# Aggregation passes of a four-layer graph network: 64 gather buffers in the feature buffer, indices copied 32 at a time, one-hots made eight in one instruction

## The reference

```python
# GCN, twice:  h = h @ W
agg = jax.ops.segment_sum(h[src] * norm[:, None], dst, num_segments=n)
# SAGE, once:  hn = layernorm(h) * gamma + beta
msg_sum = jax.ops.segment_sum(hn[src], dst, num_segments=n)
out = hn @ W_self + (msg_sum / jnp.maximum(deg, 1.0)[:, None]) @ W_neigh + b
```

## Time and profile before

| | us |
|---|---|
| median of the runs | 18431.7 |
| span of the profiled execution (first to last instruction) | 21138.5 |
| three aggregation passes in it (13177 to 15662, 15807 to 18300, 18564 to 21052) | about 7470 |
| two attention passes in it (759 to 3800, 4160 to 7050) | about 5900 |
| edge network in it (7490 to 12830) | about 5300 |
| the last block in it (21052 to 21138.5) | about 87 |

### The profile page before, as it was taken

One profiled execution on the slowest core, in us unless ns is written; L12 is line 12 of the kernel. 1 busy time (PEld: TensorE's weight loads), 2 busy tenths in 40 slices (PEclk: granted clock), 3 DMA queues, 4 the chain that ended last, 5 costly groups with the idle time before them and its releaser, 6 DMA issues. The chain is left out here.

```text
span 21138.5 us, 217919 instructions
## 1 busy us (share of the span) xinstructions
PE 9540.9 (45%) x37741; PEld 7773.1 (37%) x37741; DVE 8097.6 (38%) x29032; ACT 1416.9 (7%) x3852; POOL 12654.5 (60%) x12031
## 2 busy tenths in 40 slices
PE   0333333322222278888888885333333333333334
PEld 0222222222222266666666663232322332223233
DVE  6344444343434533333333334333333333543334
ACT  0000000000000111111111111000000000000000
POOL 1555555355555268888888882666646666356665
PEclk6555555555555566666666667555555555555556
DMA  2321221311111255555555553111121111111111
GB/s 70 57 48 48 48 48 46 48 38 40 38 39 38 62 108 106 106 106 106 106 106 106 106 105 95 44 44 44 44 68 44 44 44 44 40 51 44 44 44 48
DMA packets 1753968, 1328.70 MB, mean 63 GB/s; under 512 B 528762, under 2 KB 1576227, under 8 KB 1750312
## 3 DMA queue, kind: packets, MB, share of 16 engines
q0 software_dynamic: 570240, 778.48, 18.2%
q1 hardware_dynamic: 1182704, 530.37, 10.0%
q10 hardware_dynamic: 728, 17.33, 0.2%
HBM read 1134.48 MB, written 230.11 MB: 65 GB/s over the span
## 5 line engine op out<-in xcount | busy, mean ns | idle before, releaser
L692 POOL DMA_INDIRECT wk<-tab,idx x4992 | 4782.6, 958 | 3237.1 <-ACT idx L682 1767.1
L704 PE MATMUL PS<-wk 128*128 128x128 f32 x9984 | 2731.3, 445 | 4889.3 <-DVE wk L716 3724.4
L854 POOL DMA_INDIRECT hs<-tab_g,wk x3328 | 3232.1, 971 | 2663.0 <-ACT wk L815 1650.2
L704 PEld LDWEIGHTS PS<-wk 128*128 128x128 f32 x9984 | 2241.0, 319 | 5380.3 <-DVE F L726 3232.2
L1471 POOL DMA_INDIRECT agg<-F x1664 | 2632.9, 1582 | 515.0 <-issue 505.2
L918 PE MATMUL PS<-wk,hs 128*128 128x128 f32 x6656 | 1628.7, 416 | 2738.3 <-DVE wk L939 1302.6
L726 DVE TENSOR_TENSOR F<-F,PS 128x128 f32 x4992 | 1442.5, 289 | 3638.0 <-issue 1626.0
L918 PEld LDWEIGHTS PS<-wk,hs 128*128 128x128 f32 x6656 | 1379.9, 302 | 2991.3 <-DVE wk L939 1348.3
L1460 POOL DMA_INDIRECT F<-tab,idx x1664 | 1642.9, 987 | 720.5 <-issue 487.5
L960 DVE TENSOR_TENSOR F<-F,PS 128x126 f32 x3328 | 952.0, 286 | 2310.0 <-issue 1773.6
L716 DVE TENSOR_SCALAR wk<-iota_row,locT 128x128 f32<-128x128 f32 x4992 | 1240.2, 304 | 1154.0 <-issue 1120.2
(11 more groups left out here) (287 smaller groups left out, 8190.1 us busy)
## 6 DMA issues: line engine op xcount, KB each, us to landing
F<-src_d SPq DMA_DIRECT2D x416, 256.0 KB
F<-loc_rows_d SPq DMA_DIRECT2D x416, 256.0 KB
F<-tab_b SPq DMA_DIRECT2D x1664, 64.0 KB
wk<-tab,idx POOLq DMA_INDIRECT x4992
hs<-tab_g,wk POOLq DMA_INDIRECT x3328
F<-tab,idx POOLq DMA_INDIRECT x1664
agg<-F POOLq DMA_INDIRECT x1664
F<-agg SPq DMA_DIRECT2D x56, 448.0 KB
```

The lines of the kernel that those rows point to most:

```text
L692: pool.indirect_dma_start(gbuf[j], None, table, bass.IndirectOffsetOnAxis(idx[:, j:j + 1], 0))\
L704: pe.matmul(bank(j % 8, P), gbuf[j], onehot[j], start=True, stop=True).then_inc(summed.sem, 1)
L854: pool.indirect_dma_start(gt[s][:, j, :], None, table, bass.IndirectOffsetOnAxis(bidx[s][:, j:j + 1], 0))\
```

## The change

- `gbuf` becomes a ring of RING = 64 tiles in `hs` (the whole of the first 8192 columns). `hs` is overwritten by each pass.
- `idx` becomes 64 columns; ACT copies 32 columns at a time, once the matmuls of 32 tiles before have freed that half.
- POOL waits for the indices once in 32 tiles, and before each group of 8 gathers for `summed` of the group whose buffers it reuses, 8 groups back. The 8 gathers of a group count on one semaphore.
- PE does its waits once in 8 tiles (all 8 gathers, the one-hots of the group, the adds of the group before last) and signals once, behind the eighth matmul. The results lie in 16 tiles of 128 columns, four to a bank.
- DVE makes the 8 one-hots of a group in one `tensor_tensor` with two broadcast inputs, and waits once for the 8 matmuls before the 8 adds. The adds stay as they are.
- The loop has 26 iterations of 64 tiles.
- The last block no longer finds the own rows in `hs`: ACT issues a DMA for each node group that brings them from `tab`, one group ahead, in code that is written out instead of a loop.
- LEAD, by which all semaphores are raised at the start, is 64 instead of 16.

```diff
-LEAD = 16
+LEAD = 64
+RING = 64
...
-        gbuf = [wk[:, j * P:(j + 1) * P] for j in range(2 * HALF)]
-        onehot = [wk[:, (2 * HALF + j) * P:(2 * HALF + j + 1) * P] for j in range(2 * HALF)]
+        gbuf = [hs[:, j * P:(j + 1) * P] for j in range(RING)]
+        onehots8 = [wk[:, b * HALF * P:(b + 1) * HALF * P] for b in range(2)]
...
-                            act.wait_ge(summed.sem, summed.after(k0 - HALF))
-                            act.copy(idx[:, b * HALF:(b + 1) * HALF], srcT[:, bass.ds(k0, HALF)]).then_inc(idx_ready.sem, 1)
+                            act.wait_ge(summed.sem, summed.after(i * RG + u * (RG // 2) - RG // 2))
+                            act.copy(idx[:, u * HALF_RING:(u + 1) * HALF_RING], srcT[:, bass.ds(i * RING + u * HALF_RING, HALF_RING)])\
+                                .then_inc(idx_ready.sem, 1)
...
-                            pool.wait_ge(idx_ready.sem, idx_ready.after(i * 2 + b + 1))
+                            if g % (RG // 2) == 0:
+                                pool.wait_ge(idx_ready.sem, idx_ready.after(i * 2 + g // (RG // 2) + 1))
+                            pool.wait_ge(summed.sem, summed.after(i * RG + g + 1 - RG))
...
-                            pe.wait_ge(gathered[j].sem, gathered[j].after((i + 1) * 16))
-                            pe.wait_ge(onehot_ready.sem, onehot_ready.after(k + 1))
-                            pe.wait_ge(added.sem, added.after(k - 7))
-                            pe.matmul(bank(j % 8, P), gbuf[j], onehot[j], start=True, stop=True).then_inc(summed.sem, 1)
+                            pe.wait_ge(gathered[g].sem, gathered[g].after((i + 1) * (16 * HALF)))
+                            pe.wait_ge(onehot_ready.sem, onehot_ready.after(q + 1))
+                            pe.wait_ge(added.sem, added.after((q - 1) * HALF))
+                            for j in range(HALF):
+                                c = (g % 2 * HALF + j) * P
+                                last = pe.matmul(PS[:, c:c + P], gbuf[g * HALF + j], tile_of(onehots8[g % 2], j),
+                                                 start=True, stop=True)
+                            last.then_inc(summed.sem, 1)
...
-                            for j in range(HALF):
-                                v.tensor_scalar(onehot[b * HALF + j], iota_row[:, :], locT[:, bass.ds(k0 + j, 1)], None,
-                                                ALU.is_equal).then_inc(onehot_ready.sem, 1)
+                            v.tensor_tensor(onehots8[g % 2].rearrange("p (j c) -> p j c", c=P),
+                                            iota_row[:, :].unsqueeze(1).broadcast_to([P, HALF, P]),
+                                            locT[:, bass.ds(k0, HALF)].unsqueeze(2).broadcast_to([P, HALF, P]),
+                                            ALU.is_equal).then_inc(onehot_ready.sem, 1)
...
+                            v.wait_ge(summed.sem, summed.after(q + 1))
                             for j in range(HALF):
                                 cols = F[:, bass.ds(first_dst[j], P)]
-                                v.wait_ge(summed.sem, summed.after(k0 + j + 1))
...
-                        act.wait_ge(pe_a.sem, pe_a.after(q - 1))
-                        act.copy(ost[b], hs[:, bass.ds(q * GW, GW)]).then_inc(brought.sem, 1)
+                def own_rows(q):
+                    act.dma_start(group(ost[q % 2]), tab[q * GW:(q + 1) * GW, :].rearrange("(i p) f -> p i f", p=P))\
+                        .then_inc(more_in[q % 2].sem, 16)
+                own_rows(0)
+                for q in range(NG):
+                    b = q % 2
+                    act.wait_ge(pe_b.sem, pe_b.after(q - 1))
+                    act.copy(fT[b], F[:, q * GW:(q + 1) * GW]).then_inc(brought.sem, 1)
+                    act.wait_ge(pe_a.sem, pe_a.after(q))
+                    if q + 1 < NG:
+                        own_rows(q + 1)
```

More of the change, by code:

```diff
@@ L676, in _ @@
                 def _(act):
-                    with act.Fori(0, EI) as i:
-                        for b in range(2):
-                            k0 = i * (2 * HALF) + b * HALF
-                            act.wait_ge(summed.sem, summed.after(k0 - HALF))
-                            act.copy(idx[:, b * HALF:(b + 1) * HALF], srcT[:, bass.ds(k0, HALF)]).then_inc(idx_ready.sem, 1)
+                    with act.Fori(0, NR) as i:
+                        for u in range(2):
+                            act.wait_ge(summed.sem, summed.after(i * RG + u * (RG // 2) - RG // 2))
+                            act.copy(idx[:, u * HALF_RING:(u + 1) * HALF_RING], srcT[:, bass.ds(i * RING + u * HALF_RING, HALF_RING)])\
+                                .then_inc(idx_ready.sem, 1)
@@ L684, in _ @@
                 @block.gpsimd
                 def _(pool):
-                    with pool.Fori(0, EI) as i:
-                        for b in range(2):
-                            pool.wait_ge(idx_ready.sem, idx_ready.after(i * 2 + b + 1))
+                    with pool.Fori(0, NR) as i:
+                        for g in range(RG):
+                            if g % (RG // 2) == 0:
+                                pool.wait_ge(idx_ready.sem, idx_ready.after(i * 2 + g // (RG // 2) + 1))
+                            pool.wait_ge(summed.sem, summed.after(i * RG + g + 1 - RG))
@@ L690, in _ @@
                             pool.sem_inc(idx_taken.sem, 1)
-                            for j in range(b * HALF, (b + 1) * HALF):
+                            for j in range(g * HALF, (g + 1) * HALF):
                                 pool.indirect_dma_start(gbuf[j], None, table, bass.IndirectOffsetOnAxis(idx[:, j:j + 1], 0))\
-                                    .then_inc(gathered[j].sem, 16)
+                                    .then_inc(gathered[g].sem, 16)
                 @block.tensor
                 def _(pe):
-                    with pe.Fori(0, EI) as i:
-                        for j in range(2 * HALF):
-                            k = i * (2 * HALF) + j
-                            pe.wait_ge(gathered[j].sem, gathered[j].after((i + 1) * 16))
-                            pe.wait_ge(onehot_ready.sem, onehot_ready.after(k + 1))
-                            pe.wait_ge(added.sem, added.after(k - 7))
-                            pe.matmul(bank(j % 8, P), gbuf[j], onehot[j], start=True, stop=True).then_inc(summed.sem, 1)
+                    with pe.Fori(0, NR) as i:
+                        for g in range(RG):
+                            q = i * RG + g
+                            pe.wait_ge(gathered[g].sem, gathered[g].after((i + 1) * (16 * HALF)))
[6 more added lines that the diff above has]
+                            last.then_inc(summed.sem, 1)
@@ L709, in _ @@
                         linker(v)(v.memset(F[:, :], 0.0))
[L710 to L714, removed]
-                            for j in range(HALF):
-                                v.tensor_scalar(onehot[b * HALF + j], iota_row[:, :], locT[:, bass.ds(k0 + j, 1)], None,
-                                                ALU.is_equal).then_inc(onehot_ready.sem, 1)
+                    with v.Fori(0, NR) as i:
+                        for g in range(RG):
+                            q = i * RG + g
+                            k0 = i * RING + g * HALF
+                            v.wait_ge(summed.sem, summed.after(q - 1))
+                            v.tensor_tensor(onehots8[g % 2].rearrange("p (j c) -> p j c", c=P),
+                                            iota_row[:, :].unsqueeze(1).broadcast_to([P, HALF, P]),
+                                            locT[:, bass.ds(k0, HALF)].unsqueeze(2).broadcast_to([P, HALF, P]),
+                                            ALU.is_equal).then_inc(onehot_ready.sem, 1)
                             _, first_dst = nc.values_load_multi_w_load_instructions(
@@ L720, in _ @@
                                 skip_runtime_bounds_check_because="dst holds node numbers")
+                            v.wait_ge(summed.sem, summed.after(q + 1))
                             for j in range(HALF):
                                 cols = F[:, bass.ds(first_dst[j], P)]
-                                v.wait_ge(summed.sem, summed.after(k0 + j + 1))
+                                c = (g % 2 * HALF + j) * P
                                 v.wait_ge(added.sem, added.after(k0 + j))
[L726 to L729, removed]
+                                v.tensor_tensor(cols, cols, PS[:, c:c + P], ALU.add).then_inc(added.sem, 1)
+            for s in gathered[0:RG]:
+                s.passed(16 * HALF * NR)
+            summed.passed(NR * RG)
             added.passed(K)
-            onehot_ready.passed(K)
-            idx_ready.passed(2 * EI)
+            onehot_ready.passed(NR * RG)
+            idx_ready.passed(2 * NR)
         def attention(heads, table, ald_table, ex, whole_rows):
@@ L1855, in _ @@
             def _(act):
-                with act.Fori(0, NG // 2) as i:
-                    for b in range(2):
```

(7 more changed lines are left out.)

9 lines of the change are left out of this document (6 added, 3 removed).

## The result

The changed kernel takes 18863.74 us (median of 4 runs, 18855.6 to 18871.51), the kernel before beside it 18427.3 us (4 runs): a ratio of 1.0236, 95% interval 1.0221 to 1.025. That is 436 us more, where 101 were forecast; the time lies just above the range of 18395 to 18860. The profiled run took 18855.6 us itself, its span is 18853.7.

The account below looks back on a forecast made before the run. The prediction took POOL's gathers to bound the passes, without stalls in timed runs. Its terms summed as 18431.7 + 18 (tails) + 80 (contention) + 3 (last block) = 18532.7 us, +0.55%, range 18395 to 18860.

Parts of the forecast that it names:

- The bound: Aggregation passes: in timed runs POOL issues gathers every 1.26 us without a stall, 2097 us a pass, and bounds them.
- an observer that slows DVE: Profile against timed runs: recording each instruction slows DVE and causes POOL's waits, making the span 2706.8 us longer.
- Ring, copies, waits: POOL and ACT in the passes: no stalls to remove, added instructions hide under gathers; 0 us, at most 187.
- the round of DVE and PE: One group's one-hots, matmuls and adds take 9.1 us against POOL's 10.08 for 8 gathers; costs 0 us.
- tails: End of each pass, last gather to last add: 5.9 us longer, +18 us over three passes.
- the last block: Own rows now loaded by DMA: all loads hidden except the first, +3 us; +28 if all 14 were late.
- C: Rival: POOL's waits are real in timed runs, so 17447 us, or about 18397 if an eighth is real; chance 0.15.
- E: Rival: the round of DVE and PE exceeds 10.08 us, for example 10.4; about 18720 us; chance 0.06.
- F: Rival: the ring doesn't work as one, POOL waits at L692, time near 18450 us; chance 0.22 together with B.
- B: Rival: POOL-bound without contention, only tails and first load cost; 18453 us, no measurable change; chance 0.22 with F.
- DVE and POOL side by side: One-hots beside gathers: the two-input instruction slows gathers by 97 us, 15 saved from the old one; net +80 us.
- Rival D: The two-input one-hot instruction holds a gather for most of its length in every group; 18843 us; chance 0.09.

Follow-up runs that it names:

- h1: The kernel before, unchanged, profiled on a chip of the first kind (about 18420 us); 18419.8 us, one run.
- g1: The kernel before, unchanged, profiled on a chip of the second kind; 21161.01 us, one run.
- f2: The changed kernel with a group's one-hots again made by eight TENSOR_SCALAR instructions, first kind of chip; 18433.88 us, 1.0006 of the kernel before.
- f4: The kernel before with only a group's one-hots made by one TENSOR_TENSOR of 1024 elements, first kind of chip; 18455.82 us, 1.0018 of the kernel before.
- f3: The changed kernel with the one-hot instruction's first input, the row 0 to 127, read from PSUM, first kind of chip; 18394.78 us, 0.9985 of the kernel before.
- h2: The changed kernel with eight TENSOR_TENSOR one-hots of 128 elements, both inputs in SBUF, first kind of chip; 18449.61 us, 1.0016 of the kernel before.
- g2: The changed kernel with eight TENSOR_TENSOR one-hots of 128 elements, both inputs in SBUF, second kind of chip; 23215.23 us, 1.0977 of the kernel before.

## Why the prediction was wrong

**The bound.** That POOL's waits inside the passes are missing from the timed runs, and that the passes are POOL's, was right: h1 shows them gone. Its span is 2720.5 us shorter than that of the earlier trace rows, near the 2705.9 that were worked out, though not term by term: the two waits for ACT fall by 1178.6 and 1631.7 us, and the gathers of the attention passes take 3359.7 us instead of 3232.1. The cause given, an observer that slows DVE, was wrong. The profile must have come from a chip of the second kind, for there the unprofiled runs take 21150 us too, and g1 repeats its waits. For the time of the result this made no difference; it made the expected span wrong (20150 us against 18853.7), and it did the harm of the next-but-one point.

**Ring, copies, waits; the round of DVE and PE; tails; the last block.** Priced at 0 + 0 + 18 + 3 us; f2, which has all of them and not the instruction, measures +12 (interval of the ratio 0.9996 to 1.0015). The round: from PE's start at 13510.44 to the next one-hots at 13517.59 there are 7.15 us, with the one-hots' 1.22 and about 0.2 to PE 8.6; 9.1 were reckoned. PE waits for the gathers' DMA, and no gather for PE longer than its usual gap. Rivals C, E and F fell with POOL's waits, B with the gathers of 1046 ns.

**DVE and POOL side by side: the step that failed.** It was priced at +80 us, 97 for the new instruction less 15 for the old, and measures +439 in the gathers (5222.4 - 4783.4), 470 less 31. The 955 ns from which the 15 came stand in no row; without any hold a gather takes 951 or 952. Put into the sum in place of the 80, the 439 give 18892 us, 28 above the median. The term was formed in two wrong ways.

First, from the wrong rows. The 0.087 us per us of the earlier trace rows is a mean over a pass in which POOL stood waiting for 872 us, on a chip where DVE ran late. The same comparison in h1 is 1059 ns against 962 in the second attention pass: 97 ns x 1571 = 152 us over 329.4 us of L946, 0.46 us per us, five times as much. With it the step would have been some 340 us (774 x 0.46, less 15) and the forecast about 18800. A contention rate is only worth something from a stage in which the engine that suffers is busy as it will be.

Second, a mean over short instructions can't price a long one. The price is the rest of the instruction at the moment at which the next gather starts, less about 0.13 us. Had the 1.22 us instruction come at any time of the 1.26 us pitch alike, the mean would be 1.09 x 1.09 / 2 / 1.26 = 0.47 us, 294 us in all. It was 0.753, because the times aren't alike: the one-hots follow the adds, these the matmuls, these the group's last gather (the wait in front of PE's row, ended by the DMA), so each round puts the instruction at the same place. In 389 of 624 groups it starts 1.0 to 1.2 us after a gather's start, just ahead of the next gather, which then waits for nearly the whole of it. Mean hold by that distance, over all groups: 0.08 us at 0.2, 0.39 at 0.5, 0.69 at 0.8 and 0.97 at 1.1. In f4's kernel the phase is kinder and the same instruction cost 64 us.

The right row was there: 2.32 us in the earlier trace rows was put aside as rare. It fits the same sum, 1053.11 + 3.12 - 1054.74 + 0.83 = 2.32. Rival D named the mechanism and took half the length plus 0.3, 0.6 us a group; 0.753 was measured, and its 18843 us lie 21 below the median. In part that is luck: it was short by 80 us in the hold and left out the 31 us that go with the old instruction. It had a chance of 0.09.

The Trainium skill, "SBUF — State Buffer" (terms), describes the port shared by VectorE and GpSimd as locked for the full instruction. The gathers of 1.97 us agree with it, and f3's 951 ns agree with "GPSIMD Engine Reference" (key points), which names two SBUF inputs as one of its conditions. The prediction set that rule against a mean and believed the mean; the single row that bore it out should have counted for more.

**What stays open.** What makes DVE's register instructions last up to 1.4 us on the second kind of chip, 16 to 20 us into an unbroken stream of gathers, wasn't found. Nor why a run of short two-input instructions can hold a gather to its end in the first attention pass (the row of h1; of the gathers in h1 that met such a run with more of it to come, 120 waited for its end and 78 only for the instruction that was running) but not in h2, where the same number follow each other as closely: in h2 each has a register computation of its own ahead, and the operands differ; the two weren't tried apart.

## What to carry to other kernels

Where POOL issues gathers without a pause, count every DVE instruction that reads two tensors from SBUF, and TENSOR_SCALAR as used here, as a lock of its own length on a gather that starts inside it; one of its inputs in PSUM takes the lock away, here at no cost to DVE (1220 ns either way). Work out the phase, not the mean: loops that are fed by the gathers meet them at the same point each time. And hold a profile's span against the timed runs before reading its waits: if they are far apart, the stage rows, contention rates too, describe another machine.

## What the runs showed of the hardware

- A gather (128 rows of 128 floats here) that starts while DVE reads two inputs from SBUF ends 0.83 us after that instruction (579 of 579 in the changed kernel); alone it takes 0.952. One that runs already isn't touched, and one that starts within some 0.04 us of the instruction's start goes free while the instruction takes up to 0.08 us longer.
- With one of the two inputs in PSUM, a DVE instruction of the same length (1220 ns) holds none: gathers at 951 ns (f3).
- TENSOR_SCALAR with its tensor and its scalar column in SBUF holds by the same sum (477 of 485 gathers in h1). It lasts 0.2 to 0.3 us, so eight a group cost a gather 8 to 9 ns in the mean (f2 960 against f3 951 ns).
- Chips differ: the same kernel takes 18411 to 18435 us on one kind and 21126 to 21275 on the other, and a change worth 1.0016 on one (h2) is 1.0977 on the other (g2).
